# Masked attention in other slots, a fourth exponentials buffer, the top-2 low half ahead of the index cast, and the mask diagonal built in body 15

## What is computed

```
x = x + tanh(gx0) * attn16(LN(x), ctx)             # 16 heads of 16
x = x + tanh(gf0) * top2_experts(LN(x))            # 8 experts, weights over all 8 gates
x = x + tanh(gx1) * attn16(LN(x), ctx, mask)       # scores clipped to +-100, then masked
x = x + tanh(gf1) * top2_experts(LN(x))            # weights over the two kept gates
x = x + tanh(gx2) * attn16(LN(x), ctx)
x = x + tanh(gf2) * dense_experts(LN(x))
x = x + tanh(gx3) * attn1(LN(x), ctx)              # one head
x = x + tanh(gf3) * fp4_ffn(LN(x))
```

## Time and profile before

| | us |
|---|---|
| median of 3 runs | 1421.56 (1420.64 to 1423.65) |
| the profiled execution's own time | 1424.57 |
| its span | 1422.8 |
| TensorE matmul busy | 1310.8 (92%) |
| VectorE busy | 1104.2 (78%) |
| ScalarE busy | 693.6 (49%) |
| POOL busy | 413.8 (29%) |

### The profile page before, as it was taken

The page is one execution under the profiler, slowest core; times in us unless marked ns, Lnnn a source line. Parts: engine busy times, 40 slices in busy tenths (PEclk is TensorE's granted clock), DMA queues, the critical chain, the costliest instruction groups (busy, mean ns, idle before and its releaser), DMA issues. The chain is left out here.

```text
span 1422.8 us, 36363 instructions
## 1 busy us (share of the span) xinstructions
PE 1310.8 (92%) x11864; PEld 972.9 (68%) x11864; DVE 1104.2 (78%) x3711; ACT 693.6 (49%) x1639; POOL 413.8 (29%) x580
## 2 busy tenths in 40 slices
PE   5999999799889999999889989999988998997998
PEld 3777888644457776676544468888877887885766
DVE  7798778588778988888678867677664886668997
ACT  2666677544345555555433347676663223332322
POOL 2334346244443344447134423332330000000000
PEclk7999999999999999999889999999999998999999
DMA  5544455231333323334111143333345451451000
GB/s 166 158 121 113 137 145 155 74 116 45 93 88 98 95 81 87 91 82 121 30 50 48 58 112 96 107 88 95 100 130 164 161 170 37 132 153 33 15 15 23
DMA packets 134073, 138.11 MB, mean 97 GB/s; under 512 B 38601, under 2 KB 121292, under 8 KB 133836
## 3 DMA queue, kind: packets, MB, share of 16 engines
q1 hardware_dynamic: 133948, 136.51, 33.4%
HBM read 100.98 MB, written 35.48 MB: 96 GB/s over the span
## 5 line engine op out<-in xcount | busy, mean ns | idle before, releaser
L1135 DVE TENSOR_REDUCE negm<-ps 112x1 f32<-112x375 f32 x512 | 260.2, 541 | 106.7 <-PE ps L1259 104.8
L845 ACT ACTIVATE p<-ps 125x448 f32<-125x448 f32 x432 | 229.3, 543 | 181.1 <-PE ps L1287 109.3
L1259 PE MATMUL ps<-kst,qst 96*112 96x375 f16 x768 | 229.6, 334 | 16.1 <-DVE negm L1135 8.3
L1274 PE MATMUL ps<-qst,kst 112*125 112x224 f16 (+1 forms) x1152 | 210.0, 264 | 8.3 <-POOL qst L817 4.3
L817 POOL TENSOR_TENSOR qst<-m_row,diag 16x448 f16<-16x448 f16 x128 | 130.0, 1043 | 278.5 <-ACT m_row L924 273.5
L1274 PEld LDWEIGHTS ps<-qst,kst 112*125 112x125 f16 (+1 forms) x1152 | 148.0, 138 | 43.6 <-issue 9.3
L1767 PE MATMUL ps<-fw,xs_e 128*128 128x512 f16 x672 | 164.8, 384 | 0.0
L1131 DVE CUSTOM_DVE_ANT_0 with_mask<-ps,mask_add 112x375 f16<-112x375 f32 x256 | 135.9, 546 | 20.9 <-issue 19.8
L1119 DVE TENSOR_SCALAR ps<-ps 125x448 f32<-125x448 f32 x192 | 120.8, 629 | 26.8 <-PE ps L1274 25.4
L1259 PEld LDWEIGHTS ps<-kst,qst 96*112 96x112 f16 x768 | 97.2, 130 | 44.4 <-DVE negm L1135 20.9
L1182 PE MATMUL ps<-wkv_split,ctxT 128*125 128x256 f16 x864 | 120.1, 276 | 1.1 <-DVE ks L1090 1.1
(11 more groups left out here) (259 smaller groups left out, 2397.5 us busy)
## 6 DMA issues: line engine op xcount, KB each, us to landing
k_split<-ks SPq DMA_DIRECT2D x48, 375.0 KB, 3.6
kst<-k_split SPq DMA_DIRECT2D x96, 187.5 KB, 2.9
fw<-in_w SPq DMA_DIRECT2D x16, 1024.0 KB, 7.2
qst<-q_split SPq DMA_DIRECT2D x96, 112.0 KB, 2.4
kst<-k_split SPq DMA_DIRECT2D x96, 93.8 KB, 2.6
stage<-in_ctxT SPq DMA_DIRECT2D x16, 375.0 KB, 3.9
ctxn<-in_ctx SPq DMA_DIRECT2D x16, 375.0 KB
rows<-x SPq DMA_DIRECT2D x48, 112.9 KB, 2.4
```

The lines of the kernel that those rows point to most:

```text
L845: act.activation(p[P_OF[hg]][:, kt, :], ps[0:KR, BK_ST + n % 2, 0:4 * S], ACT.Exp).then_inc(s_exp, 1)
L1135: dve.tensor_reduce(g.negm[1 - par][:, h:h + 1], scored, AX_X, ALU.max, negate=True).then_inc(s_max, 1)
L1259: mm = pe.matmul(ps[0:S, BK_S + h % 2, 0:SK], g.q_stack[q][0:96, h, :], g.k_stack[q][0:96, h // 2, :], start=True, stop=True)
L1274: mm = pe.matmul(bank[:, 2 * r * S:2 * (r + 1) * S], g.k_stack[par][0:rows, pr, kt * KR:(kt + 1) * KR], g.q_stack[par][0:rows, 2 * pr:2 * ...
```

## The change

1. **Slots of the masked layer.** `PLANS[True]` is another table. W0 moves from slot 10 to 12, W2 from 23 to 28, the rows R from 1 to 6, the scores end in slot 19 instead of 22, TW moves from 12 to 11, the last values from 26 to 22, `xn` from 31 to 29 and `m_row` from 27 to 31 on ScalarE, the update of `x` from 18 to 22.
2. **A fourth buffer in the unmasked layers.** Group 3 goes to `m_stack` (free there) instead of buffer 0. An exponential waits for the previous body's weighing of its own group, checked at each group's first third.
3. **`weigh` without `more`:** W2 waits for its own exponentials alone.
4. **`mask_diagonal` in body 15** of layer 0 instead of body 3.
5. **Top-2:** the subtraction of the low half stands in front of the cast of the indices.

```diff
-P_OF = (0, 1, 2, 0)
...
-    True: Plan(turned=[0, 2, 4, 6, 8, 10, 12, 14, 16, 18, 20, 22], shift=[2, 4, 6, 9, 10, 12, 14, 16, 18, 20, 24, 24],
-               scores=[0, 1, 2, 4, 5, 9, 9, 11, 14, 14, 16, 17, 18, 19, 20, 22], weigh=[10, 14, 23, 30], keys=[1, 4],
-               low=[1, 7], rows=1, q=7, values=[17, 20, 26], turn=12, divide=12, back=16, out=19, update=18,
-               stats=[22, 23, 23], maxima=29, pv=6, split=29, split_low=17, norm=31, xnT=4, q_out=9, k_out=[3, 6],
-               v_out=[17, 20, 26], oT=14, m_out=27),
+    True: Plan(turned=[0, 2, 4, 6, 8, 10, 12, 14, 16, 18, 20, 22],
+               shift=[2, 4, 6, 9, 10, 12, 14, 17, 18, 20, 23, 24],
+               scores=[0, 1, 2, 4, 4, 9, 9, 10, 11, 13, 13, 15, 16, 17, 18, 19], weigh=[12, 14, 28, 30], keys=[1, 4],
+               low=[0, 4], rows=6, q=7, values=[17, 20, 22], turn=11, divide=12, back=16, out=19, update=22,
+               stats=[23, 26, 30], maxima=30, pv=0, split=30, split_low=16, norm=29, xnT=5, q_out=9, k_out=[1, 4],
+               v_out=[17, 20, 25], oT=16, m_out=31),
...
+    p_of = (0, 1, 2, 0) if clipped else (0, 1, 2, 3)
+    if not clipped:
+        p.append([g.m_stack[kt // 2][0:KR, :, :].rearrange("p h s -> p (h s)").bitcast(F32)
+                  [:, kt % 2 * 4 * S:(kt % 2 + 1) * 4 * S] for kt in range(KT)])
...
-                if first and isinstance(i, int) and i == 3:
-                    pool.wait_ge(s_mstack, 5 * HG)
+                if first and isinstance(i, int) and i == B - 1:
+                    pool.wait_ge(s_mstack, B * HG)
                     mask_diagonal()
...
-                if n == 0:
-                    at_least(act, s_pv, i * HG)
-                if kt == 0 and hg == 3:
-                    at_least(act, s_pv, i * HG + 1)
+                if kt == 0 and clipped:
+                    at_least(act, s_pv, i * HG + max(hg - 2, 0))
+                elif kt == 0:
+                    if first and isinstance(i, int) and n == 9 and i == 0:
+                        act.wait_ge(s_zdram, 32)
+                    at_least(act, s_pv, (i - 1) * HG + hg + 1)
...
-                pe.wait_ge(s_exp, i * ST_SLOTS + (hg + 1 + more) * KT)
+                pe.wait_ge(s_exp, i * ST_SLOTS + (hg + 1) * KT)
...
+                    if tiled(i + 2):
+                        dve.wait_ge(s_xhi, i + 3)
+                        dve.tensor_tensor(xs[par][:, 1, :, :], turned, xs[par][:, 0, :, :], ALU.subtract)\
+                            .then_inc(s_xlo, 1)
                     if gates:
                         step.after(picked)
                         step(dve.tensor_copy(indexf[:, :], index[:, 0:2]))
...
-                    if tiled(i + 2):
-                        dve.wait_ge(s_xhi, i + 3)
-                        dve.tensor_tensor(xs[par][:, 1, :, :], turned, xs[par][:, 0, :, :], ALU.subtract)\
-                            .then_inc(s_xlo, 1)
```

More of the change, by code:

```diff
@@ L564, in attention @@
     local = ExitStack()
-    p = g.p + [local.enter_context(nc.sbuf_tensor(f"p2_a{layer}", [KR, KT, 4 * S], F32))]
+    p_of = (0, 1, 2, 0) if clipped else (0, 1, 2, 3)
+    p = [[t[:, kt, :] for kt in range(KT)]
+         for t in g.p + [local.enter_context(nc.sbuf_tensor(f"p2_a{layer}", [KR, KT, 4 * S], F32))]]
+    if not clipped:
+        p.append([g.m_stack[kt // 2][0:KR, :, :].rearrange("p h s -> p (h s)").bitcast(F32)
+                  [:, kt % 2 * 4 * S:(kt % 2 + 1) * 4 * S] for kt in range(KT)])
     mask_d = a["mask"]
@@ L839, in take_exp @@
                 act.wait_ge(s_st, i * ST_SLOTS + n + 1)
-                if n == 0:
-                    at_least(act, s_pv, i * HG)
-                if kt == 0 and hg == 3:
-                    at_least(act, s_pv, i * HG + 1)
-                act.activation(p[P_OF[hg]][:, kt, :], ps[0:KR, BK_ST + n % 2, 0:4 * S], ACT.Exp).then_inc(s_exp, 1)
+                if kt == 0 and clipped:
[4 more added lines that the diff above has]
+                    at_least(act, s_pv, (i - 1) * HG + hg + 1)
+                act.activation(p[p_of[hg]][kt], ps[0:KR, BK_ST + n % 2, 0:4 * S], ACT.Exp).then_inc(s_exp, 1)
             def context_high(turn):
@@ L1288, in shift_and_mask, with weigh @@
                           start=False, stop=True, skip_group_check=True).then_inc(s_st, 1)
-            def weigh(i, par, hg, more):
-                pe.wait_ge(s_exp, i * ST_SLOTS + (hg + 1 + more) * KT)
+            def weigh(i, par, hg):
+                pe.wait_ge(s_exp, i * ST_SLOTS + (hg + 1) * KT)
                 if hg == 0:
@@ L1298, in weigh @@
                         mm = pe.matmul(pv[32 * j:32 * j + 32, hg * S:(hg + 1) * S], g.v[par][:, kt, 4 * hg + j, :],
-                                       p[P_OF[hg]][:, kt, j * S:(j + 1) * S], start=(kt == 0), stop=(kt == KT - 1))
+                                       p[p_of[hg]][kt][:, j * S:(j + 1) * S], start=(kt == 0), stop=(kt == KT - 1))
                 mm.then_inc(s_pv, 1)
@@ L1360, in body @@
                     if on["e"] and s in plan.weigh:
-                        for n, hg in enumerate(plan.weigh[s]):
-                            weigh(i, par, hg, len(plan.weigh[s]) - 1 - n)
+                        for hg in plan.weigh[s]:
+                            weigh(i, par, hg)
             schedule(Steps(pe, s_s), 0, body)
```

## The result

| us | before | after |
|---|---|---|
| median | 1421.6 (4 runs) | 1411.0 (4 runs, 1409.07 to 1413.1) |
| the profiled execution | 1424.57 | 1411.63 |
| its span | 1422.8 | 1409.8 |

The changed kernel takes 0.9915 of the time before (95% interval 0.9896 to 0.9934), 12.1 us less (9.4 to 14.8). The forecast was 1413.6 us in a range of 1408.5 to 1420.5.

A forecast was written before the change was run, and what follows sets the result against it. TensorE was taken as the bound, VectorE close behind. Masked layer -4.7, diagonal -1.7, W2 and W3 in body 15 -0.6, top-2 -1.0 summed to -8.0 us: 1413.6 us from the 1421.56 median, range 1408.5 to 1420.5.

The forecast's parts named there:

- masked layer: New slot table: 0.4 us less a body over 14 masked bodies, less small costs: -4.7 us, between 0 and -12.
- top-2: Top-2 parts: of TensorE's waits for the low half, at most 7.7 us, -1.0 us, between -4 and +4.
- R, 0.3 us: Masked body: R takes 0.30 us in slot 1; in slot 6 it stands where TensorE waits for clip 2 anyway.
- S6, 0.44 gained and 0.2 back at S5: Masked body: W0 and two scores fill the wait before S6, 0.44 us gained; W0 missing before S5 costs 0.2.
- VectorE leads in slots 9 to 19, S7 stands 0.3 us: Masked body: VectorE's 10.0 us there against TensorE's about 8; S7 stands some 0.3 us, repaid at the body's end.
- W3, 0.2 lost: Masked body's end: W3 needs exponential 11 and comes no earlier, with W2 now as cover: 0.2 us lost.
- The diagonal, no cost, at most 0.8: Layer 0, body 15: POOL may hold up small VectorE steps, but slack covers it; whole diagonal term -1.7 us.
- The weights come later, as just fits: Top-2 tiles: weights come about 1 us later, at 359.6; TensorE turns them at 359.97.
- VectorE leads: Rival, chance 0.17: in masked bodies, dense slots 9 to 19 cost what the rest gives; masked layer 0, total 1418.3 us.
- more than reckoned: Rival, chance 0.08: in masked bodies S4 and S7 don't wait either; -0.85 us a body, -15 us, 1406.
- Maxima late: Rival, chance 0.08: row maxima 0.8 us late, S0 stands 0.6 us; 0.2 us more a masked body, total 1421.0.
- Weights late: Rival, chance 0.07: in top-2 tiles, weights queued behind the moved subtraction exceed the tile by 0.5 us; +6 us, 1427.

## Why the prediction was right, and where it wasn't

The sign, the place and the order of size held: the time comes from TensorE's standing in the masked layer. By steps (us in the traces):

| step | forecast | measured |
|---|---|---|
| masked layer | -4.7 | -8.1 (13 bodies) |
| diagonal | -1.7 | -1.4 at the old place, +1.2 at the new |
| W2 and W3 in body 15 | -0.6 | -0.4 each, -0.8 |
| top-2 | -1.0 | +0.4 and -2.7, -2.3 |
| sum | -8.0 | -11.4; by device time -12.1 (-9.4 to -14.8) |

The total lies in the range partly by luck: the masked layer and the top-2 parts were put 3.4 and 1.3 us too low, the diagonal 1.5 too high. Of the 0.34 us a body that I summed for the table, 0.64 were measured:

- *R, 0.3 us*: mis-sized, and the largest miss. Up to S2 the change is 0.48 us ahead. Some 0.2 of it is what R costs in slot 1 of the new table; the rest is R's wait for `xn` in the old one, which I had not reckoned. It stays won because ScalarE's copies moved as well.
- *S6, 0.44 gained and 0.2 back at S5*: the size held (0.26 for both, with the three scores more between T5 and S6 reckoned in), but my reason, W0, was wrong by the run with W0 in slot 10 (0.06 us). The scores do it.
- *VectorE leads in slots 9 to 19, S7 stands 0.3 us*: this failed as a mechanism. I counted 10.0 us of VectorE's work against 8 of TensorE's. But only five clips stand in slots 9 to 19 (T5 to T9 in 10 to 18), not seven, and reciprocal and division take 0.63 us to the next start (506.57 to 507.20), not 0.8: 5.3 + 2.75 + 0.63 = 8.7 us. TensorE's steps from the first of these scores to behind the last take 8.6 (499.10 to 507.73). In the body shown, from the first of the 11 maxima to the end of the last, both are busy for 98% and neither leads (the row below, columns as in the earlier trace rows). S7 also moved behind T8, the turning back and a score, which I left out. The wait exists (0.51 us in front of S7) where the dense scores come without the later shift, and not in the change. Reckoned by starts and scores, the stretch from S6 to S8 still loses 0.2 us, where 0.3 was forecast.

```profile
499.64:508.49 8.85, 8.65 (x96) 6.64 (x97) 8.70 (x41) 4.30 (x11) 2.13 (x5) 1.00 0.41 109
```

- *W3, 0.2 lost*: not so. It is 0.57 us from S10 to W2 and 0.91 more to W3 in the new body, 1.48 in all, where I had kept 1.61 and a wait on top.
- *The diagonal, no cost, at most 0.8*: this step failed. I named the collision and its size, two to three times up to 1.8 us, and then trusted the update's idle of 1.22 us. That idle was read in an execution in which TensorE was late by a slow weighing; without it the update had 0.46 us (the run with the table alone). The term is -0.2, not -1.7.
- *The weights come later, as just fits*: TensorE doesn't wait for them. My one cast of 0.16 us was half of the picture: in the middle tiles of the first part casts of 0.16 and of 0.7 us took turns, in tiles of 6.1 to 6.2 and of 6.5 to 6.6. In the change nearly every one there takes 0.36 to 0.40, in tiles of 6.4 to 6.6, and nothing is gained. VectorE stands for ScalarE's high half in three of the 11 tiles (0.63, 0.63 and 0.47 us); what the 0.4 us of this part are made of stays open. In the second part I said that VectorE's chain bounds and leaves nothing; but that chain itself has become shorter by the cast's 0.35 us, 0.2 net, which I had left out: the cast's 0.56 us stood in the trace of before, beside an addition of POOL.

Of the rivals, *VectorE leads* is no error of thought but a near neighbour: the scores one slot earlier, or without the later shift, give it (19.55 and 19.91 us). Of *more than reckoned* half came: S7 doesn't wait, S4 does as before (0.20 us in the body shown), and the body lost 0.64 us where that rival had 0.85. *Maxima late* did not occur: S0 (494.59) does not wait for `mst` in a steady body. *Weights late* did not either.

## What to carry over

- Two engines that are busy for 94% and 88% of a loop are balanced by order: what decides is which instructions stand between a product and the one that needs its clip, and the moves pay only together. Half of a table can lose what the whole of it gains.
- Look in the trace for short VectorE steps that take several times their usual length, and for what POOL does then. Moving either pays in one chain (0.35 us in the cast, 0.2 net in a tile) and costs in another (1.2 us).
- Count the steps of each engine in a stretch one by one before calling one of them the leader: two clips too many and a few rounded costs made a lead of 2 us out of one of 0.1.
- Before an idle time is taken as slack, see whether it was made by something that another execution doesn't have.

## Not expected of the hardware

- VectorE steps of 0.15 to 0.42 us last up to the end of the POOL instruction beside them or a little beyond: the cast 0.58 instead of 0.22 us, the mask conversion 1.28 instead of 0.42 (0.2 us beyond it), the steps of the root 1.74 instead of 0.17. In the last case it is also a `TENSOR_TENSOR` on SBUF alone. None of the 192 clips on PSUM took longer than 0.63 us, before or after.
- The same weighing takes 1.35 or 0.78 us in one and the same place, by run, with a granted clock of 0.53 or 1.00 behind the same three waits, and the stretch around it is 1.4 us longer in the first case. That is more than two of the four parts of this change are worth, so a single profile can't weigh them; distances that leave such a stretch out can.
- In one run the matmuls were two to three times as long while the record granted full speed. Its cause stays open.
